# Row maxima over two banks at a time, and another order of the attention stage, in a cross-attention and feed-forward layer

## The reference

```python
x = x + diff_attention(layernorm(x), ctx, ctx)   # 16 heads of 32, 8 key/value heads
x = x + ffn(layernorm(x))
# diff_attention: two score sets per head, from the two halves of q and k
w = softmax(q1 k1^T) - lam * softmax(q2 k2^T)    # over 154 keys
attn = rms_norm(w v) * g * (1 - LAMBDA_INIT);  out = attn @ Wo.T
# ffn: hidden 2048, ternary weights w1, w2
h = gelu(layer_norm(x) @ tern(w1).T + b1);  out = layer_norm(h) @ tern(w2).T + b2
```

## Time and profile before

| | |
|---|---|
| median of 3 runs | 2534.48 us (2524.53 to 2538.64) |
| profiled execution | 2503.8 us, of which the span is 2502.0 |
| PE busy | 2206.3 us (88%) |
| DVE busy | 1858.1 us (74%) |
| ACT busy | 1517.3 us (61%) |
| POOL busy | 1032.3 us (41%) |
| mean granted TensorE clock | 0.929 of full speed |

### The profile page before, as it was taken

One profiled execution on the slowest core, in us unless ns is written; L12 is line 12 of the kernel. 1 busy time (PEld: TensorE's weight loads), 2 busy tenths in 40 slices (PEclk: granted clock), 3 DMA queues, 4 the chain that ended last, 5 costly groups with the idle time before them and its releaser, 6 DMA issues.

```text
span 2502.0 us, 45089 instructions
## 1 busy us (share of the span) xinstructions
PE 2206.3 (88%) x18239; PEld 1206.5 (48%) x18239; DVE 1858.1 (74%) x3030; ACT 1517.3 (61%) x1973; POOL 1032.3 (41%) x803
## 2 busy tenths in 40 slices
PE   7678989898988989899898988989898898989878
PEld 5444455454545545455454545545454544545443
DVE  3776779687787968778686777868777787877763
ACT  3674657665565756556665655666566566665554
POOL 2302607154270714527062451805336180633507
PEclk9868999999998999999899999999999998999989
DMA  7313131120412213131231313113141212212010
GB/s 290 103 49 83 25 89 48 44 81 27 105 35 85 51 44 77 31 86 39 70 81 37 84 31 81 44 52 81 31 109 31 81 44 62 75 33 71 14 39 17
DMA packets 253007, 160.14 MB, mean 64 GB/s; under 512 B 171812, under 2 KB 221580, under 8 KB 252288
## 3 DMA queue, kind: packets, MB, share of 16 engines
q1 hardware_dynamic: 249792, 152.07, 22.6%
q0 software_dynamic: 3008, 5.20, 0.7%
HBM read 51.82 MB, written 20.38 MB: 29 GB/s over the span
## 4 chain that ended last, share of the span: by engine, by line
PE 54%; DVE 26%; ACT 10%; issue 6%; DMA 3%; SPq 1%; POOL 1%; DVEq 0%; POOLq 0%; ACTq 0%
PE ps L1583 10%; PE ps L1599 8%; DVE arena L1105 8%; PE ps L1430 6%; PE ps L1431 6%; PE ps L1432 5%; DVE arena L1221 5%; ACT p L812 3%; PE ps L1518 3%; PE ps L1609 3%; ACT arena L809 3%; PE ps L1486 3%; DVE arena L1098 2%; DMA stack_raw<-row_words 2%; ACT arena L807 2%
## 5 line engine op out<-in xcount | busy, mean ns | idle before, releaser
L685 POOL TENSOR_TENSOR attn_raw<-attn_raw 128x512 f32<-128x512 f32 x448 | 642.8, 1454 | 49.5 <-ACT attn_raw L837 21.1
L663 POOL TENSOR_TENSOR q<-q 128x512 f16<-128x512 f32 x128 | 168.6, 1322 | 913.0 <-ACT q L798 911.7
L1583 PE MATMUL ps<-rows,w1T 128*128 128x512 f16 x2048 | 485.2, 380 | 2.2 <-DVE rows L1216 2.2
L1105 DVE TENSOR_REDUCE arena<-ps 128x3 f32<-128x462 f32 (+1 forms) x704 | 402.3, 613 | 33.1 <-PE ps L1486 32.5
L1221 DVE SCALAR_TENSOR_TENSOR arena<-attn_raw,vec_cols,arena 128x512 f16<-128x512 f32 x256 | 291.9, 1140 | 54.6 <-ACT arena L835 51.4
L807 ACT ACTIVATE arena<-ps 128x1024 f32<-128x1024 f32 x128 | 130.9, 1023 | 321.3 <-PE ps L1518 321.3
L1599 PE MATMUL ps<-w2T,arena 128*128 128x512 f16 x1200 | 303.5, 406 | 0.0
L832 ACT ACTIVATE attn_raw<-ps,vec_cols,wstep 128x512 f32<-128x512 f32 x256 | 198.4, 775 | 151.4 <-PE ps L1583 149.4
L1583 PEld LDWEIGHTS ps<-rows,w1T 128*128 128x128 f16 x2048 | 192.4, 97 | 193.4 <-DVE rows L1216 2.7
L1127 DVE TENSOR_TENSOR p<-arena,p 128x1024 f16<-128x1024 f32 (+1 forms) x128 | 190.9, 1492 | 116.0 <-ACT p L812 106.7
L1127 DVE TENSOR_TENSOR attn_raw<-arena,attn_raw 128x1024 f16<-128x1024 f32 (+1 forms) x128 | 189.2, 1489 | 97.5 <-ACT attn_raw L812 90.6
(11 more groups left out here) (191 smaller groups left out, 4581.6 us busy)
## 6 DMA issues: line engine op xcount, KB each, us to landing
stack_raw<-q SPq DMA_DIRECT2D x744, 64.0 KB, 2.0
arena<-in_x SPq DMA_DIRECT2D x64, 256.0 KB, 2.8
out<-arena SPq DMA_DIRECT2D x64, 256.0 KB, 2.0
arena<-in_x SPq DMA_DIRECT2D x14, 1024.0 KB, 5.4
arena<-in_L_ffn_w SPq DMA_DIRECT2D x7, 1024.0 KB, 13.8
rows<-in_x SPq DMA_DIRECT2D x2, 1024.0 KB, 6.7
stack_raw<-in_L_xattn_Wq SPq DMA_DIRECT2D x8, 256.0 KB, 9.2
k_att<-k_store SPq DMA_DIRECT2D x4, 495.0 KB
```

Source lines behind the costliest of these rows:

```text
L685: ins = pool.tensor_tensor(acc[:, e, :], acc[:, e, :], src[:, j % NG, :], ALU.add)
L1105: dve.tensor_reduce(negmax[:, tt, u0:u1], ps[:, row_bank(c, tb), 0:(u1 - u0) * S].rearrange("p (u s) -> p u s", s=S), AX.X, ALU.max, negat ...
L1583: ins = pe.matmul(ps[:, B_H + j % 2, :], w1T[:, k, j * P:(j + 1) * P], rows16[:, e, k, :], start=(k == 0 and e == 0), stop=(k == KD - 1 an ...
```

## The change

`row_max_pair` reduces two neighbouring banks with one instruction (for blocks from 2 on), so a bank's step now waits for the pair before the last. `MAXIMA_AT` has even numbers, with none beside the last hidden step, and `split_maxima` stands behind `gelu_lo` of step 14 (`TLAST`) instead of 15. `ATTEND` has another order, and tile 1's late product is cut into two parts instead of three. The condition in PE's `iteration` gives the same banks for the same steps as before.

```diff
 ATTEND = [(w[0], int(w[1:] or 0)) for w in (
-    "e1 c g e2 s0 e3 y0 y1 q0 s1 h1 v0 z0 z1 s2 h2 v1 y2 s3 q1 t0 z2 v2 s4 h3 v3 s5 h4 t1 y3 v4 s6 q2 z3 v5 s7 t2 q3 v6 v7").split()]
-LATE1 = 8
-LATE = {("e", 1): (1, LATE1, 12), ("e", 2): (1, 12, 15), ("e", 3): (1, 15, JH),
+    "c e1 g y0 y1 s0 e2 q0 s1 v0 h1 s2 h2 y2 v1 s3 q1 t0 z0 z1 v2 s4 h3 v3 s5 h4 y3 t1 v4 s6 q2 z2 z3 v5 s7 q3 v6 t2 v7").split()]
+LATE = {("e", 1): (1, 8, 12), ("e", 2): (1, 12, JH),
         ("h", 1): (2, 0, 8), ("h", 2): (2, 8, JH), ("h", 3): (3, 0, 8), ("h", 4): (3, 8, JH)}
-MAXIMA_AT = (1, 2, 2) + (3,) * (JH - 3)
-TLAST = JH - 1
+MAXIMA_AT = (2, 2, 2, 4, 2, 4, 4, 2, 4, 2, 4, 4, 2, 4, 2, 0)
+TLAST = JH - 2
...
+            def row_max_pair(c, tb):
+                b, tt = divmod(tb, TT)
+                u0, u1 = UPB * b, min(UPB * b + UPB, UNITS)
+                bank = row_bank(c, tb)
+                wait(dve, s_t, c, NT, tb + 2)
+                dve.tensor_reduce(negmax[:, tt:tt + 2, u0:u1],
+                                  ps[:, bank:bank + 2, 0:(u1 - u0) * S].rearrange("p b (u s) -> p b u s", s=S),
+                                  AX.X, ALU.max, negate=True).then_inc(s_tmax, 2)
+
+            def row_maxima(c, tbs):
+                if c < 2:
+                    for tb in tbs:
+                        row_max(c, tb)
+                else:
+                    for tb in tbs[::2]:
+                        row_max_pair(c, tb)
...
                 for j in range(JH):
-                    for tb in beside[:2]:
-                        row_max(i + 1, tb)
+                    row_maxima(i + 1, beside[:2])
                     gelu_lo(i, j)
-                    for tb in beside[2:]:
-                        row_max(i + 1, tb)
+                    row_maxima(i + 1, beside[2:])
...
                 if tb >= row_banks(c):
-                    wait(pe, s_tmax, c, NT, tb - row_banks(c) + 1)
+                    wait(pe, s_tmax, c, NT, tb - row_banks(c) + (1 if c < 2 else 2 - tb % 2))
...
-                        ffn_step(i, j - FLAG, banks if j - FLAG >= LATE1 or not ahead else (2, 3))
+                        ffn_step(i, j - FLAG, (2, 3) if ahead and j - FLAG < JH // 2 else banks)
```

## The result

The changed kernel takes 2397.86 us (median of 4 runs, 2393.09 to 2405.18), the kernel before 2529.51 in the same comparison (2520.22 to 2538.64). The ratio is 0.948, with a 95% interval of 0.944 to 0.953: 5.2% or 132 us less. The forecast was 2402, so the total is 4 us off. The profiled execution is at 2394.91 with a span of 2393.1; it gained 109 on its own predecessor, where 132 was forecast.

What follows compares the result with a forecast made beforehand. The order of work was taken to bound the kernel: six TensorE waits (15.1 us per iteration) and slow clock after them. 14 x 9 = 126, with the last iteration 132, off 2534.5 gave 2402 us; range 2348 to 2495.

Steps and rivals of the forecast that it cites:

- Pairs: Row maxima on VectorE: 44 reductions become 22 of 1.03 us each, saving 1.4 us of VectorE time.
- End of the stage: End of feed-forward: transposes of the maxima at 1025.4 instead of 1026.7, first scores (s0) 1.4 us earlier.
- s1: Second group of scores in attention: with y0, y1 ahead of `probs_lo(0)`, it starts 4.1 us earlier in all.
- rival A: Slow clock moves, over s1 and h1 and at the feed-forward stage's end: 5 us gained per iteration, 2458 us; chance 0.2.
- v0 before h1: Attention after s1: new 0.6 us wait for `probs_lo(0)`, but the 1.2 GHz stretch goes (3.2); 6.7 us in all at s2.
- y2: y2 before v1 in attention: q1's 2.5 us wait and its slow clock (1.6) go; 10.8 us in all.
- Behind s4: Late attention: 0.9 us won at v7, out-projection takes about 0.7 back, some 1.8 off for collisions; 9 us per iteration.
- The step from the profile to the median: Whole kernel: median of the runs stays 30.7 us above the profiled execution, so 2372 becomes 2402 us.
- Rival B: Attention: VectorE replaces TensorE as limit, half the gain after s2 returns as `probs_lo` waits; 3 us per iteration, 2492; chance 0.1.

## Why the prediction was right, and where it was not

The direction, the place and the order of size were right, and the total too, but not by its own sum. How much earlier each point comes, counted from the first hidden step of the feed-forward stage (14 iterations of the profiled executions):

| gain in all, us | forecast | median | mean |
|---|---|---|---|
| transposes of the maxima | 1.3 | 1.9 | 1.8 |
| s0 | 1.4 | 1.4 | 1.8 |
| s1 | 4.1 | 2.9 | 3.5 |
| s2 | 6.7 | 5.9 | 5.3 |
| group 4 (behind q1) | 10.8 | 10.0 | 9.6 |
| v7 | 11.7, less up to 1.8 | 8.5 | 8.3 |
| period | 9 | 7.9 | 7.7 |

*Pairs: right.* Where pairs stand back to back, one starts 1.03 us after the one before it, as worked out from 0.07 fixed; and the instruction is worth some 9 us in all, where 1.4 an iteration (20) was forecast. The Trainium skill ("VectorE: DVE Perf Modes", section "The TRN2 errata — SBUF-src ops pay a fixed extra latency per instruction") gives 120 cycles and one per element for a source in PSUM; an estimate by that is 1.09 for a pair. A pair's own duration is 1.107 (median), near it; for the distance of two starts the measurement decides for 1.03.

*End of the stage: the place right, the reason incomplete.* The transposes come 1.9 earlier, where 1.3 was forecast, and the way from them to s0 takes 5.3 instead of the 4.9 that it kept, so s0 gains its 1.4. The forecast charged the split to DVE, gave the gain to the pairs and saw `MAXIMA_AT` only as where reductions stand. The runs show the opposite shares: pairs 9 us, places some 34. With the new order, what the places save is the wait for the split, 23.2 us in 13 iterations of the order alone and none with single reductions in the new places, and the slow clock behind it over e1 and g.

*s1: a term mis-sized.* 4.1 was forecast, and 2.9 is the median. That s1 waits for q0's end and not for y1 was right; the step that failed is that q0 begins at s0 + 3.2. It begins 3.1 after s0 in 4 of the 14 iterations, 4.5 to 4.6 in 8 and 5.8 in 2, because s0 or e2 runs at the 1.2 GHz level. Where the clock stays full, s1 comes 5.7 after s0, and 5.8 was forecast. That is a piece of rival A, given a chance of 0.2 as a whole: the slow clock did partly move, and the mean clock is 0.940, not the 0.96 forecast. Where it starts stays open. It isn't the wait for `gelu_lo(15)`: with that wait filled e2 is slow in every iteration. What PE does before e2 is g, 16 matmuls with one column each, the wait for s0's DMA, and s0; before the change, e2 stood ahead of s0. No run moved e2 alone.

*v0 before h1: wrong as a step.* The forecast had it cost a wait of 0.6. The swap itself is worth nothing. The slow clock that the forecast credited to this place did go (h1 5.57 to 3.61), and stays away with h1 ahead of v0, so it went with the waits before s1.

*y2: right.* 2.5 + 1.6 was forecast; undone, it lengthens the way from s3 to s4 by 4.2 and the period by 4.1.

*Behind s4.* The forecast had 0.9 more at v7, less 0.7 at the out-projection and 1.8 for collisions. Of the 10.0 gained at s4, 8.5 are left at v7 and 7.9 at the next hidden step. `probs_lo(7)` takes 3.83 instead of 2.88 beside GpSimd's q_lo(3), an overlap that t2 had before, and the out-projection waits for t2's DMA.

*The step from the profile to the median: wrong, and it paid for the rest.* The forecast kept 30.7 us between the profiled execution and the median. It is 3 in the changed kernel. 14 x 1.3 = 18 us too much gain per iteration and 5 in the last, against 28 of an offset that went away. That the two cancel is luck. The offset was no property of the launch: the profiled execution of the kernel before was faster than all its others, as the last section shows.

*Rival B* was priced wrongly: half of the gain after s2 (4.1 of the 10.8) coming back leaves some 7 per iteration, not 3, and its time would be nearer to the forecast's than 2492. PE's waits for `probs_lo` are 2.1 us in 13 iterations, so it did not happen.

## What to carry to other kernels

An in-order engine's list decides who waits: a short operation whose result frees a bank for the bottleneck belongs ahead of long ones that have slack, and each such swap is read off the chain of waits and priced as its wait plus the slow matmuls behind it. Ask of a moved step what used to cover the one it exposes: the order alone left some 30 to 40 us behind, because the transposes now stood before a split that came too late. Hold medians against medians: one profiled execution of a kernel that scatters by 2% can hide a gain of 1%. Before filling a wait or raising the clock, look for the wait right behind it; here it took the whole gain.

## What the runs showed of the hardware that was not expected

The scatter of a kernel can go with its TensorE clock. Single executions of the kernel before took 2550.9 us at a mean granted clock of 0.903, 2544.8 at 0.909, 2534.4 at 0.912, 2516.2 at 0.923 and 2508.0 at 0.924; its profiled execution, 2503.8, had 0.929. The eight executions of the changed kernel lie between 2393.1 (0.943) and 2405.2 (0.936), 12 us apart, where those of the kernel before are 47 apart. The same program has more or fewer slow stretches from run to run. A part of this lies between comparisons: the seven executions of one lie between 2538.0 and 2550.9, the seven of another between 2508.0 and 2539.0. It is not the waits alone that make the scatter: the kernel with the pairs and their places alone has as many of them (170.7 us of PE's waits between 400 and 2200 us, 170.0 before), and its ten executions lie within 6.4 us, at 0.925 to 0.930. Why an execution falls at one end or the other was not tried. It does mean that the gain read between two profiled executions, 109, was less than that between medians, 132.
